# A fused early-fusion layer with eight experts on one Trainium2 core: new places for the end of attention, the routing and the last three expert blocks

## What is computed

```python
h = concatenate([patches @ W.T + b, (weight_l @ weight_r)[x_txt]], axis=1)   # 16 x 68 x 256
n = layernorm(h)
q, k, v, a = n @ W_q, n @ W_k, n @ W_v, sigmoid(n @ W_gate + b_gate)
S = a * S + k * v ; o = q . S                                                # per step and head
h = h + o @ W_o
n = layernorm(h)
probs = softmax(n @ Wg); top_vals, top_idx = top_k(probs, 2); top_vals /= sum(top_vals)
h = h + sum over the two experts e of top_vals * (relu(n @ W1[e] + b1[e]) @ W2[e] + b2[e])
```

## Time and profile before

| what | us |
|---|---|
| median of 3 runs | 353.27 |
| the three runs | 346.86, 353.27, 354.75 |
| the profiled execution | 350.91 |
| its span in the trace | 349.0 |

### The profile page before, as it was taken

One profiled execution on the slowest core, in us unless ns is written; L12 is line 12 of the kernel. 1 busy time (PEld: TensorE's weight loads), 2 busy tenths in 40 slices (PEclk: granted clock), 3 DMA queues, 4 the chain that ended last, 5 costly groups with the idle time before them and its releaser, 6 DMA issues.

```text
span 349.0 us, 8036 instructions
## 1 busy us (share of the span) xinstructions
PE 324.4 (93%) x2819; PEld 299.6 (86%) x2820; DVE 199.8 (57%) x421; ACT 143.8 (41%) x329; POOL 150.4 (43%) x220
## 2 busy tenths in 40 slices
PE   8888999999999999999997999988959999999883
PEld 7568989999999999999995887877849999999862
DVE  2056298757586874879783125687733464444333
ACT  1158653352434335252423245412633745456311
POOL 5881225143134322223116494657053666666311
PEclk9999999999999999999998999999998999999999
DMA  6991006023030240000000004125663776877167
GB/s 170 275 288 48 2 12 233 2 90 107 2 107 0 60 169 2 0 2 3 3 0 2 0 2 152 48 71 175 205 207 123 200 249 196 251 208 252 49 198 246
DMA packets 18469, 38.45 MB, mean 110 GB/s; under 512 B 2753, under 2 KB 9922, under 8 KB 18306
## 3 DMA queue, kind: packets, MB, share of 16 engines
q1 hardware_dynamic: 16002, 31.43, 29.5%
q0 software_dynamic: 2432, 6.56, 5.8%
HBM read 32.60 MB, written 5.37 MB: 109 GB/s over the span
## 4 chain that ended last, share of the span: by engine, by line
PE 75%; DVE 9%; DMA 7%; issue 4%; SPq 2%; ACT 1%; DVEq 0%; POOL 0%; ACTq 0%; POOLq 0%
PE ps L949 10%; PE ps L520 8%; PE ps L694 7%; PE ps L710 7%; PE ps L787 7%; PE ps L522 7%; PE ps L521 7%; PE ps L962 3%; PE ps L674 3%; PE ps L964 3%; PE ps L963 3%; DMA pt<-patches 3%; PE ps L675 2%; PE ps L676 2%; DMA xg<-xrows,gather_u 2%
## 5 line engine op out<-in xcount | busy, mean ns | idle before, releaser
L1374 DVE RECIPROCAL invU<-U 128x272 f32<-128x272 f32 x32 | 57.8, 1829 | 0.0
L520 PE MATMUL ps<-xnhi,wlo 128*128 128x272 f32 x192 | 57.6, 300 | 0.0
L522 PE MATMUL ps<-xnhi,whi 128*128 128x272 f32 x192 | 55.3, 288 | 0.0
L521 PE MATMUL ps<-xnlo,whi 128*128 128x272 f32 x192 | 55.2, 288 | 0.0
L1781 POOL TENSOR_TENSOR qA<-qraw,invU 128x544 f32<-128x544 f32 x16 | 22.4, 1402 | 72.8 <-DVE invU L1374 37.9
L949 PE MATMUL ps<-xt,w 128*128 128x128 f32 x384 | 48.3, 280 | 2.7 <-DVE xt L1645 1.1
L949 PEld LDWEIGHTS ps<-xt,w 128*128 128x128 f32 x384 | 46.1, 196 | 3.4 <-issue 2.4
L1381 DVE TENSOR_TENSOR pb<-ps,causal 128x592 uint32<-128x592 uint32 (+3 forms) x32 | 27.4, 856 | 31.1 <-PE ps L694 30.9
L1883 POOL DMA_INDIRECT yrows<-yb,scatter_u x24 | 25.1, 1045 | 46.7 <-DVE yb L1662 35.7
L1232 ACT ACTIVATE hr<-ps,b 128x128 f32<-128x128 f32 x96 | 27.4, 368 | 34.2 <-PE ps L949 33.7
L787 PE MATMUL ps<-wo,oT 128*128 128x264 f32 x144 | 37.9, 404 | 0.6 <-ACT oT L1115 0.6
(11 more groups left out here) (226 smaller groups left out, 653.5 us busy)
## 6 DMA issues: line engine op xcount, KB each, us to landing
w<-w SPq DMA_DIRECT2D x32, 512.0 KB, 4.0
wraw<-w_attn SPq DMA_DIRECT2D x8, 384.5 KB, 3.3
yin<-yrows SPq DMA_DIRECT2D x8, 256.0 KB, 4.4
pt<-patches SPq DMA_DIRECT2D x5, 288.0 KB, 5.7
wv<-w_v SPq DMA_DIRECT2D x4, 256.0 KB, 3.0
oT<-w_ot SPq DMA_DIRECT2D x1, 1024.0 KB, 11.9
wo<-w_o SPq DMA_DIRECT2D x2, 512.0 KB, 12.4
b<-b SPq DMA_DIRECT2D x1, 1024.0 KB, 5.3
```

Source lines behind the costliest of these rows:

```text
L520: pe.matmul(dst, slo, mhi[n], start=(i == 0), stop=False)
L521: pe.matmul(dst, shi, mlo[n], start=False, stop=False)
L522: last = pe.matmul(dst, shi, mhi[n], start=False, stop=(i == len(pairs) - 1))
L1374: dve.reciprocal(invU[:, g * GT:(g + 1) * GT], U[:, g * GT:(g + 1) * GT]).then_inc(s_a, 1)
```

## The change

- TensorE at the end of attention: `out_part(0, 0, 7)` stands ahead of the last mix of pair 6 and of the range product, and waits for 15 of the 16 query copies; the 16th is waited for ahead of the last pair's first mix. `out_part(0..3, 7, 8)` wait only for the first two groups of the last pair (s_o 30), the rest is waited for ahead of `out_part(4)`. ScalarE splits two more experts ahead of that mix's copy.
- Routing: `read_table` becomes `read_rows` (gather rows) and `read_places` (scatter rows); `read_rows(0)` runs right behind `choose_full`, `read_rows(1)` ahead of `split_h(1)`. Tiles 6 and 7 are marked by GpSimd instead of VectorE. `copy_x(2)` and `scale_of(8)` move ahead of `find_ranks(8)`; on ScalarE the last tile's deviation, normalisation and kept row move ahead of `relu(0)` and `relu(1)`. `turn_x(2)` moves ahead of `up(1)`. The total of the first six tiles is summed from three products instead of one that waits for `add_up(5)`. SP loads w1 of block 1 when gather 0 has landed, not gather 1. On GpSimd gather 5 stands ahead of scatter 0.
- Last three blocks (BY_ACT = 3, blocks 21 to 23): the low part is made by GpSimd (s_hrlo_p), b2 is added by TensorE as a product with the identity, the result is copied out by ScalarE (`keep_y`, s_yb_a), and the blocks alternate between PSUM banks 6 and 5. VectorE waits for low_blocks and all_blocks and starts the loads with a tiny write each (s_load). The four filler products (L1021) between the second `add_rows` are gone.

```diff
@@ SP
             load_w1(0)
             keep_rows(6)
             sp.wait_ge(s_gx[0], 16)
+            load_w1(1)
+            keep_rows(7)
             sp.wait_ge(s_gx[1], 16)
-            load_w1(1)
             load_w1(2)
-            keep_rows(7)
@@ TensorE
-            mix(HP - 2, 0, G - 1)
-            pe.wait_ge(s_okcol, 1)
-            pe.wait_ge(s_vev, VC * IT)
-            pe.matmul(ps[0:1, 6, 0:1], ok_col[:, 0:1], ones[:, 0:1], ...).then_inc(s_okmm, 1)
...
-            pe.wait_ge(s_qraw, 2 * HP)
+            pe.wait_ge(s_qraw, 2 * HP - 1)
             pe.wait_ge(s_o, 4 * (HP - 2) + 2)
             out_part(0, 0, HP - 1)
+            mix(HP - 2, 0, G - 1)
+            pe.wait_ge(s_okcol, 1)
+            pe.wait_ge(s_vev, VC * IT)
+            pe.matmul(ps[0:1, 6, 0:1], ok_col[:, 0:1], ones[:, 0:1], ...).then_inc(s_okmm, 1)
             pair_scores(HP - 1, 1, 0)
             out_part(1, 0, HP - 1)
+            pe.wait_ge(s_qraw, 2 * HP)
             mix(HP - 1, 1, 0, bank=6)
...
-            pe.wait_ge(s_o, 4 * HP)
-            pe.wait_ge(s_p, 4 * HP)
+            pe.wait_ge(s_o, 4 * (HP - 1) + 2)
             pe.wait_ge(s_way, 1)
             for r in range(4):
                 out_part(r, HP - 1, HP)
+            pe.wait_ge(s_o, 4 * HP)
+            pe.wait_ge(s_p, 4 * HP)
             out_part(4, 0, HP)
...
+            def last_down(b, par):
+                e = expert_of(b)
+                pe.wait_ge(s_tab, 4)
+                pe.wait_ge(s_hrlo_p, b - (NB - BY_ACT) + 1)
+                if b == NB - 2:
+                    pe.wait_ge(s_yb, NB - BY_ACT)
+                if b == NB - 1:
+                    pe.wait_ge(s_yb_a, 1)
+                acc = ps[:, 5 + par, 0:D]
+                pe.matmul(acc, ident[:], b2[:, bass.ds(e, 1), :]..., start=True, stop=False)
...
             pe.wait_ge(s_owner, 2)
             block_step(2, 0)
-            pe.wait_ge(s_counted, 1)
-            low_blocks, all_blocks = (pe.value_load(filled_i[0:1, i:i + 1], ...) for i in range(PICKS))
+            pe.wait_ge(s_bias, 32)
...
-            down(NB - 3, 1)
+            last_down(NB - 3, 1)
             up(NB - 1, 1)
-            down(NB - 2, 0)
-            pe.wait_ge(s_filled, low_blocks)
-            add_hrow(0).then_inc(s_load, 1)
+            last_down(NB - 2, 0)
+            add_hrow(0)
             add_hrow(1)
             add_hrow(3)
-            down(NB - 1, 1)
-            pe.wait_ge(s_filled, all_blocks)
-            add_hrow(2).then_inc(s_load, 1)
+            last_down(NB - 1, 1)
+            add_hrow(2)
@@ VectorE
             choose_full()
+            read_rows(0)
             take_moments(6)
             choose(6)
-            read_table(0)
             tile_rest(6)
+            read_places(0)
...
             copy_x(3, 1)
+            read_rows(1)
             split_h(1, 1)
-            read_table(1)
+            read_places(1)
             add_b2(0, 0)
-            for b in range(2, NB - 2):
+            for b in range(2, NB - BY_ACT):
                 block_step(b, b % 2)
...
+            copy_x(NB - 1, 1)
+            add_b2(NB - BY_ACT - 1, 0)
+            dve.wait_ge(s_filled, low_blocks)
+            dve.memset(mark_d[:, 0:1], 0.0).then_inc(s_load, 1)
+            dve.wait_ge(s_filled, all_blocks)
+            dve.memset(mark_d[:, 1:2], 0.0).then_inc(s_load, 1)
@@ GpSimd
-            for b in range(XG):
-                gather(b)
+            gather(0)
+            gather(1)
             add_up(6)
+            gather(2)
             add_up(7)
             order_rows(6, 2)
-            gather(XG)
+            gather(3)
+            mark_places(6, 1)
             order_rows(8, 1)
-            for b in range(XG + 1, NF):
-                gather(b)
-            pool.wait_ge(s_tab, 2)
+            mark_places(7, 1)
+            gather(4)
+            pool.wait_ge(s_tab, 3)
+            pool.wait_ge(s_xlate, 16 * (RT - FT))
+            gather(NF)
             for b in range(NB):
...
-                if b + NF < NB:
+                if 0 < b < NB - NF:
                     gather(b + NF)
-                if b > 0:
-                    scatter(b)
-                if b >= 2:
+                if 2 <= b < NB - 2:
                     tell_filled(b - 2)
+                scatter(b)
+                if b >= NB - 2:
+                    tell_filled(b - 1)
+                if b >= NB - BY_ACT - 2 and b < NB - 2:
+                    if b == NB - 3:
+                        tell_filled(b - 1)
+                    split_h(b + 2, b % 2)
```

More of the change, by code:

```diff
@@ L870, in count, with slots @@
                 if r == FT - 1:
-                    pe.wait_ge(s_prev, FT)
-                    last = pe.matmul(ps[:, 7, (A + 1) * E:(A + 2) * E], ones_m[:], prev[:, FT], start=True, stop=True)
+                    for i, moved in enumerate((prev[:, r], pick[:, r, 0], pick[:, r, 1])):
+                        last = pe.matmul(ps[:, 7, (A + 1) * E:(A + 2) * E], ones_m[:], moved, start=(i == 0), stop=(i == PICKS))
                 last.then_inc(s_count, 1)
-            def slots(r0, r1, by_pool=False):
+            def slots(r0, r1):
                 part = r0 // FT
@@ L965, in down @@
                 last.then_inc(s_dn, 1)
+            def last_down(b, par):
+                e = expert_of(b)
+                pe.wait_ge(s_tab, 4)
+                if b < NB - BY_ACT:
+                    pe.wait_ge(s_hrlo, b + 1)
+                else:
+                    pe.wait_ge(s_hrlo_p, b - (NB - BY_ACT) + 1)
[4 more added lines that the diff above has]
+                acc = ps[:, 5 + par, 0:D]
+                if b >= NB - BY_ACT:
+                    pe.matmul(acc, ident[:], b2[:, bass.ds(e, 1), :].rearrange("p o n -> p (o n)"), start=True, stop=False)
+                for j in range(FC):
+                    hi, lo = (t[:, bass.ds(e, 1), j * D:(j + 1) * D].rearrange("p o n -> p (o n)") for t in (w2hi, w2lo))
+                    hhi, hlo = hrhi[par][:, j * P:(j + 1) * P], hrlo[par][:, j * P:(j + 1) * P]
+                    pe.matmul(acc, hlo, hi, start=(j == 0 and b < NB - BY_ACT), stop=False)
+                    pe.matmul(acc, hhi, lo, start=False, stop=False)
+                    last = pe.matmul(acc, hhi, hi, start=False, stop=(j == FC - 1))
+                last.then_inc(s_dn, 1)
             def block_step(b, par, one=(), two=()):
@@ L982, in _ @@
             count(8)
+            turn_x(2, 0)
             up(1, 1)
-            turn_x(2, 0)
             up(2, 0)
@@ L1020, in _ @@
             for n in range(len(TURNED)):
-                pe.matmul(ps[:, 3, 0:D], mean_w[:], first[:, 0:D], start=True, stop=True)
                 add_rows(n, 1).then_inc(s_sum, 1)
@@ L1227, in relu @@
                 act.wait_ge(s_up, b + 1)
-                if not early(b, 2):
+                if isinstance(b, int) and b - 2 >= NB - BY_ACT:
+                    act.wait_ge(s_hrlo_p, b - 1 - (NB - BY_ACT))
+                elif not early(b, 2):
                     act.wait_ge(s_hrlo, b - 1)
@@ L1605, in choose_rest, with read_rows @@
                                          ).then_inc(s_counted, 1)
-            def read_table(part):
+            def read_rows(part):
                 b, n = slice(NF * part, NB if part else NF), NR if part else NF
@@ L1695, in _ @@
             take_moments(RT - 1)
-            mark_places(6, 2)
+            copy_x(2, 0)
+            scale_of(RT - 1)
             find_ranks(RT - 1, 1)
-            copy_x(2, 0)
             mark_places(RT - 1, 1)
@@ L1714, in _ @@
                     weigh()
-            split_h(NB - 2, 0)
-            add_b2(NB - 3, 1)
-            split_h(NB - 1, 1)
-            add_b2(NB - 2, 0)
+            dve.wait_ge(s_counted, 1)
+            low_blocks, all_blocks = (dve.value_load(filled_i[0:1, i:i + 1], min_val=1, max_val=NB) for i in range(PICKS))
+            copy_x(NB - 1, 1)
[4 more added lines that the diff above has]
+            dve.memset(mark_d[:, 1:2], 0.0).then_inc(s_load, 1)
             dve.wait_ge(s_share, 1)
@@ L1723, in _ @@
                                          ALU.mult, ALU.add).then_inc(s_part, 1)
-            add_b2(NB - 1, 1)
             for n, (r, _) in enumerate(COMB):
```

50 lines of the change are left out of this document (34 added, 16 removed).

## The result

| | before | after |
|---|---|---|
| median, run beside each other | 350.61 us (346.86 to 354.75, 4 runs) | 336.99 us (336.25 to 337.93, 4 runs) |
| profiled execution: time, span | 350.91, 349.0 | 336.3, 333.9 |
| ratio after to before, 95% interval | | 0.9702 (0.9642 to 0.9761) |

The changed kernel is faster, by 13.6 us from median to median and by 10.5 us (3.0%) by the ratio. Some executions of a kernel are several us longer at a lower granted clock, and the ratios leave those out. Three of the four executions of the kernel before are those of its first table.

What follows compares the result with a forecast made beforehand. TensorE, busy in 93% of the span, was taken as the bound, with gains only where it idles or runs at half clock. 4.5 + 6.7 + 4.0 = 15.2 us off bases gave 333.8 to 338.1; forecast 337, range 331 to 343.

Steps and rivals of the forecast that it cites:

- the profiled one is as good a base as the median: Choice of base: with three runs 8 us apart, the profiled execution (350.91) serves as well as the median (353.27).
- Attention: End of attention: TensorE goes from the scores straight into `out_part(0)` at full clock; 4.5 us, between 2.4 and 5.0.
- Routing: Routing to the block loop's start: earlier tables, gather 5 ahead of scatter 0, no half clock; 6.7 us, bounds 1.4 and 8.
- `up(1)`: Routing: w1 of block 1, started by gather 0's landing, lands 3.9 us after issue, so `up(1)` comes 1.6 us earlier.
- The slack of 1.9 us that I gave gather 5: Routing: gather 5 lands at 254.2, ahead of `turn_x(5)` at 256.1.
- The count read: Ahead of TensorE's block loop: the two values read there are gone, yet 0.6 of the 1.06 us idle stays.
- End: Last three blocks: earlier loads and low parts on GpSimd bring ScalarE's last copy forward; 4.0 us, between 1 and 5.
- the writes behind it are the same: Very end: the output writes behind ScalarE's last copy stay unchanged.
- Routing giving little: Rival: added GpSimd marks or `add_b2(0)` hold the blocks; routing gives 3 us instead of 6.7, total 341; chance 0.13.
- the end giving little: Rival: GpSimd's queue becomes the bound and late low parts delay TensorE; total 340; chance 0.10.
- The clock at the end: Rival: a late second half idles TensorE and its last products run at 1.2 GHz; total 339.5; chance 0.08.
- half clock enter the block loop: Rival: TensorE stays at half clock into the block loop behind short gaps, 3.4 us more a block; 362; chance 0.03.

Runs made afterwards that it cites:

- `route_alone`: The kernel before with only the routing part of the change, TensorE's read of the two counts kept: 351.47 us, ratio 0.9891 to the kernel before.
- `attn_alone`: The kernel before with only the new order at the end of attention: 352.69 us, ratio 0.9911 to the kernel before.
- `last_three_alone`: The kernel before with only the last three blocks' part of the change: 355.31 us, ratio 0.9978 to the kernel before.
- `fill_gap`: The kernel before with five unused products filling TensorE's two gaps at the end of attention: 358.92 us, ratio 1.01 to the kernel before.
- `gather5_late`: The changed kernel with gather 5 put back behind scatter 0 on GpSimd: 340.88 us, ratio 0.9794 to the kernel before.
- `values_back`: The changed kernel with TensorE's two reads of the block counts put back ahead of its block loop: 338.24 us, ratio 0.9734 to the kernel before.
- `w1_early`: The changed kernel with SP loading the weights of blocks 1 and 2 one step earlier each: 339.35 us, ratio 0.9784 to the kernel before.
- the first four experiments: The kernel before with each of the three parts alone, then with filler products, on one chip: 352.69, 351.47, 355.31 and 358.92 us.
- `best`: The changed kernel with earlier w1 loads, a reworked end and `add_b2(0)` ahead of `read_places(1)`: 341.07 us, ratio 0.9819 to the kernel before.

## Why the prediction was right, point by point

**The time.** Forecast 337.0, measured 336.99. The closeness is partly luck, for several errors partly cancelled. The sum was 15.2 us; the stretches gave 14.1, and 1.0 came from the front, where nothing was changed. The base was off as well: the kernel before ran at 350.61 beside the new one, not at 353.27. Of the 14.1, about 3.2 are half clock in the profiled execution of before: 1.65 in A (against `route_alone`) and 1.57 at `down(2)` and `up(5)` (4.89 us from 261.55 to 266.44, against 3.32 from 251.04 to 254.36). Without them 10.9 are left, near the 10.5 of the ratio. It is not in every execution of the old order, but it is no rare accident either: at `out_part(0)` it came in two traces of three, and at `up(5)` in `attn_alone` and `last_three_alone` too (3.43 and 3.38 us long), but not in `fill_gap` (1.95). The step that failed here is "the profiled one is as good a base as the median": an idle gap is in every run, the half clock behind it is not, and it should have stood in the sum with a chance.

**Attention, 4.5 forecast, 4.35 measured.** The scores of pair 7 came 4.24 earlier against 4.4, the clock was full, and the branch kept 0.52 of the 0.63 us; the sum had 0.1 for it and got 0.11.

**Routing, 6.7 forecast, 6.71 measured**, but by other pieces. In times less the 5.37 us of front and attention: gather 5 came 5.2 earlier (5.8 forecast), `down(1)` 1.1 (1.4), `up(4)` 2.3 (2.1), `turn_x(6)` 6.7 (6.9). The term that was wrong is `up(1)`: 1.6 forecast, 0.16 measured. Its weights took 5.5 us from SP's issue at 232.72 to the product, not 3.9, beside the gathers and row writes. It was cheap because what mattered was gather 5, and there `gather5_late` gives 2.6 us for its place in the queue, as the 1.61 and 1.03 of the earlier trace rows told. The open 1.03 us in front of `down(2)`, which I put down to reading the expert, shrank to 0.13 as forecast. In five of the experiments 0.5 to 0.6 of it came back: in two of them `turn_x(5)` waited 1.73 and 1.87 us for its rows, in three so little that only its length tells (0.44 instead of 0.38). The slack of 1.9 us that I gave gather 5 was not there: it is nearly zero. The count read was to leave 0.6 of 1.06; it left nothing, and `values_back` gives 0.9 to 1.1 for it. With these two and the 1.57 us of clock some 5.2 of the 6.71 are accounted for; the other 1.5 us, the earlier first table and its gathers among them, no run took back by itself.

**End, 4.0 forecast, 3.06 measured.** Low parts took 1.31, 1.28 and 1.44 us (1.28 forecast), the two triggers came 0.5 and 0.3 us ahead of the forecast, the additions ran without a wait, and ScalarE's last copy ended 3.7 us earlier than before against the start of `up(22)` (4.0 forecast). The term that failed is the last sentence, "the writes behind it are the same". They are not: ScalarE's four copies now come 0.43 us apart (the additions that each waits for came 0.87 apart before, at 342.51, 343.37 and 344.24), and SP, at 0.5 us a write, falls behind them by 0.7 us.

**The rivals.** Routing giving little and the end giving little did not come. The clock at the end did not fall, with 0.52 us of idle time before `last_down(23)` and 1.00 in all stretches; nor did half clock enter the block loop, though waits of 0.92 and 0.96 us stand before it. I had left the reverse of it out: that the kernel before would lose its half clock by itself.

## What to carry to other kernels

A transfer should be started by the engine that first knows that its data is complete, not by the one that will need it: with the triggers put back, the 3 us at the end were gone. In a queue of gathers and scatters look first at the order by due time: one place was 2.6 us. And moving large loads earlier in a queue is not free where small gathers run beside them: in `w1_early` it took away the wait that it aimed at and lost 1.6 us at the rows of gather 0. An idle gap can be counted in a sum; the half clock behind it only with a chance.

## What the hardware showed that I had not expected

- Behind the same idle time (1.08 + 1.35 us) the granted clock fell to 0.50 in two executions and stayed at 1.00 in a third; `out_part(0)` took 5.46, 5.16 and 3.77 us.
- On the chip of the first four experiments the block loop took 66.6 to 67.7 us instead of 59, with stalls of up to 1.9 us, in one of which VectorE, ScalarE and SP stood still together.
- A load of 512 KB landed after 3.9 us in the median of the changed kernel and after 5.5 us beside the first gathers; a gather of 128 rows, from its start to the turn that waited for it, took 3.2 to 4.3 us, and 5.6 (`w1_early`) and 6.3 (`best`) beside such loads.
- In one execution of `fill_gap` TensorE stopped for 1.47 us in straight code, with no releaser in the profile. The program differs from the kernel before by five products.
